# Block 1 after its attention: down weights staged earlier, first shared inputs split earlier, weight conversions set between the shared items

## What is computed

```python
xn = _layernorm(x)
s = _L1_attn_ref(xn, ...)     # 16 heads, causal softmax with ALiBi, out @ w_proj + b_proj
g = _silu(_L1_ffn_ref(xn, ...))
x = x + s * g

# _L1_ffn_ref: E = 16 experts of inner width 176, top 2 of a sigmoid router,
# and one shared expert of inner width 352 that every token passes
y0 = _mlp(xf, sw1, sw2, sw3)                  # (silu(x @ w1.T) * (x @ w3.T)) @ w2.T
for e1, e2, e3, we in experts: y = y + _mlp(xf, e1, e2, e3) * we[:, None]
```

## Time and profile before

| stretch of the span (us) | what runs | PE busy | ACT busy | DVE busy | mean granted clock |
|---|---|---|---|---|---|
| 0 to 337.0 | block 0 | 298.7 | 137.9 | 181.2 | 1.00 to 120 us, 0.95 behind |
| 337.0 to 568.9 | projections and attention of block 1 | 188.9 | 98.0 | 136.0 | 0.92 |
| 568.9 to 601.1 | tail of the last sequence, shared expert on chunk 0 | 18.2 | 12.4 | 11.0 | 0.79 |
| 601.1 to 668.0 | routed experts, first part | 66.0 | 51.6 | 44.4 | 0.97 |
| 668.0 to 745.5 | last experts, shared expert on chunks 1 to 3, combination, store | 43.9 | 31.1 | 47.8 | 0.81 |

### The profile page before, as it was taken

One profiled execution on the slowest core, in us unless ns is written; L12 is line 12 of the kernel. 1 busy time (PEld: TensorE's weight loads), 2 busy tenths in 40 slices (PEclk: granted clock), 3 DMA queues, 4 the chain that ended last, 5 costly groups with the idle time before them and its releaser, 6 DMA issues.

```text
span 745.5 us, 12625 instructions
## 1 busy us (share of the span) xinstructions
PE 615.7 (83%) x4090; PEld 481.1 (65%) x4090; DVE 420.4 (56%) x1000; ACT 331.1 (44%) x715; POOL 158.8 (21%) x164
## 2 busy tenths in 40 slices
PE   3989982999999989895728999998887589999750
PEld 2868872999988878783414666666665267776430
DVE  6166663455545374558686546555441356665468
ACT  2223321566554344433412544543444458886331
POOL 0136660000005434006002122222000100001652
PEclk9999997899999999997858999999999799999885
DMA  9904434334315111009296757658300425552324
GB/s 326 295 35 141 152 125 168 99 115 119 117 65 182 50 51 49 9 1 187 85 139 140 157 134 163 133 118 147 47 2 1 121 85 157 164 157 84 95 87 138
DMA packets 85179, 86.50 MB, mean 116 GB/s; under 512 B 19435, under 2 KB 76654, under 8 KB 84846
## 3 DMA queue, kind: packets, MB, share of 16 engines
q1 hardware_dynamic: 78462, 68.79, 35.8%
q0 software_dynamic: 6144, 16.79, 7.6%
q10 hardware_dynamic: 512, 0.13, 0.1%
HBM read 51.20 MB, written 34.21 MB: 115 GB/s over the span
## 4 chain that ended last, share of the span: by engine, by line
PE 39%; DVE 10%; ACT 5%; issue 3%; DMA 2%; POOL 0%; ACTq 0%; SPq 0%; DVEq 0%
PE bank L793 5%; PE bank L856 4%; PE bank L880 3%; PE bank L948 3%; PE bank L1015 3%; PE bank L1033 3%; PE bank L992 2%; PE bank L642 2%; PE bank L844 2%; PE bank L811 2%; PE bank L1017 2%; PE bank L994 2%; PE bank L867 1%; PE bank L972 1%; DVE mneg L1853 1%
## 5 line engine op out<-in xcount | busy, mean ns | idle before, releaser
L575 POOL DMA_INDIRECT slots<-xn,slot_of x64 | 66.4, 1037 | 183.5 <-DMA slots<-xn,slot_of 110.4
L1853 DVE TENSOR_REDUCE mneg<-bank 128x2 f32<-128x512 f32 (+1 forms) x96 | 62.5, 685 | 41.7 <-PE bank L994 41.2
L1690 DVE TENSOR_TENSOR xgl<-bank,xgh 128x256 f16<-128x256 f32 (+1 forms) x86 | 36.5, 424 | 51.2 <-ACT xgh L1276 51.2
L588 POOL DMA_INDIRECT rets<-results,slot_of x32 | 33.5, 1048 | 147.3 <-DMA results<-ys 105.9
L1664 DVE TENSOR_TENSOR hf<-bank,sg 128x512 f32<-128x512 f32 x36 | 24.6, 690 | 65.5 <-PE bank L793 60.4
L588 POOL DMA_INDIRECT gu<-results,slot_of x32 | 31.3, 978 | 121.2 <-DMA results<-ys 104.6
L844 PE MATMUL bank<-cf,xn 128*128 128x128 f32 x172 | 35.9, 292 | 14.6 <-DMA xn<-slots 12.4
L992 PE MATMUL bank<-KS,QS 99*128 99x256 bf16 (+1 forms) x256 | 37.2, 254 | 12.8 <-DVE mneg L1853 7.5
L1251 ACT ACTIVATE sg<-bank 128x512 f32<-128x512 f32 x36 | 21.2, 599 | 57.1 <-PE bank L793 57.0
L1697 DVE TENSOR_TENSOR hs<-bank,gs 128x176 f32<-128x176 f32 x86 | 29.3, 341 | 28.8 <-ACT gs L1282 24.5
L1385 ACT ACTIVATE exps_first_keys<-bank 128x512 f32<-128x512 f32 x64 | 34.7, 597 | 21.8 <-PE bank L1017 21.8
(11 more groups left out here) (234 smaller groups left out, 1637.1 us busy)
## 6 DMA issues: line engine op xcount, KB each, us to landing
xn<-slots SPq DMA_DIRECT2D x86, 128.0 KB, 2.2
results<-ys SPq DMA_DIRECT2D x86, 128.0 KB, 1.7
projection_parts<-parts SPq DMA_DIRECT2D x16, 384.0 KB, 3.2
QS<-projection_parts SPq DMA_DIRECT2D x48, 128.0 KB, 4.4
KS<-projection_parts SPq DMA_DIRECT2D x48, 128.0 KB, 6.5
slots<-zrow SPq DMA_DIRECT2D x1, 6016.0 KB, 23.8
x<-in_x SPq DMA_DIRECT2D x8, 512.0 KB, 5.9
x<-in_w SPq DMA_DIRECT2D x4, 704.0 KB, 8.1
```

The lines of the kernel that those rows point to most:

```text
L575: pool.indirect_dma_start(out=slots_dram, out_offset=bass.IndirectOffsetOnAxis(ap=at, axis=0), in_=xn[:, t, :], in_offset=None).then_inc(s ...
L588: pool.indirect_dma_start(out=rets[L][:, t % RETS, r, :], out_offset=None, in_=results_dram[L], in_offset=bass.IndirectOffsetOnAxis(ap=at, ...
L1690: dve.tensor_tensor(xgl[L][:, j % 2, :], PS[j % 2][:, 0:D], high[:, j % 2, :], ALU.subtract)\
L1853: dve.tensor_reduce(mneg[:, qt, h0:h0 + heads], PS[6 + p % 2][:].rearrange("p (n k) -> p n k", n=heads), AX.X, ALU.max, negate=True).then_ ...
```

## The change

Four things are moved, and nothing is computed otherwise.

- `dn_stage` gets four buffers and a place in SBUF where `QS`/`KS` of slot 2 lay (last used by sequence 5). SP issues all four pairs as soon as the transposed scores of sequences 0 to 5 are formed. The experts' first rows, which stand behind them in SP's queue, move along.
- `high_x(1, 0)` and `low_x(1, 0)` stand inside round 7 of the attention on ACT and DVE, and `shared_gates(1, 0)` stands on PE behind round 7 and ahead of the tail of the last sequence.
- POOL clears `dn1` after the last weighted values instead of after the last projection.
- The conversions stand between the shared items: on each engine its two L1454-like ones (128 partitions) behind item 0, its two L1455-like ones (48 partitions) behind item 1, and the split of chunk 1 (`high_x(1, 1)`, `low_x(1, 1)`) behind item 2.

```diff
-            sp.wait_ge(s_ps[1], after(NSEQ))
+            sp.wait_ge(st_ps, after(12 * (NSEQ - 2)))
             for n in range(4):
-                if n >= 2:
-                    sp.wait_ge(dn_act if n % 2 == 0 else dn_dve, n // 2)
                 e = slice(4 * n, 4 * n + 4)
-                sp.dma_start(dn_stage[:, n % 2, :, 0:D], w1_rows[0:P, e, 2 * KT * P:WCOLS]).then_inc(s_stage[n % 2], 16)
...
+                sp.dma_start(dn_stage[:, n, :, 0:D], w1_rows[0:P, e, 2 * KT * P:WCOLS]).then_inc(s_stage[n], 16)
...
             scatter(1, 1)
+            pool.wait_ge(pv_ps, after(4 * NSEQ))
+            pool.memset(dn1.bitcast(F32)[:, :, 1, :], 0.0).then_inc(dn_zero, 1)
             pool.wait_ge(s_ps[1], after(NSEQ))
             pool.memset(hs1[:, :, INNER:D], 0.0).then_inc(pads_set, 1)
-            pool.memset(dn1.bitcast(F32)[:, :, 1, :], 0.0).then_inc(dn_zero, 1)
...
             for u in range(-1, NSEQ):
                 attention(u)
+            pe.wait_ge(s_sw, 16)
+            shared_gates(1, 0)
             pe.wait_ge(s_sb[1], after(NSEQ - 1))
             heads_transposes(NSEQ - 1, 0)
...
-            shared(1, (0,), nothing)
+            shared(1, (0,), nothing, begun=True)
...
                     exp_scores(u, 3)
+                if not ahead:
+                    high_x(1, 0)
...
             outputs_copy(NSEQ - 1)
-            act.wait_ge(s_ps[1], after(NSEQ))
-            high_x(1, 0)
-            high_x(1, 1)
-            act.wait_ge(dn_zero, 1)
-            for n in (0, 2):
-                act.wait_ge(s_stage[n % 2], 32 * (n // 2 + 1))
...
+            def down_weights(k):
+
+                if k < 2:
+                    for n in (0, 2):
+                        act.wait_ge(s_stage[n], 32)
+                        if k == 0:
+                            act.activation(dn1[:, 4 * n:4 * n + 4, 0, :], dn_stage[:, n, :, 0:D], ACT.Copy)
+                        else:
+                            act.wait_ge(dn_zero, 1)
+                            act.activation(dn1[0:INNER - P, 4 * n:4 * n + 4, 1, :],
+                                           dn_stage[0:INNER - P, n, :, D:2 * D], ACT.Copy).then_inc(dn_act, 1)
+                else:
+                    high_x(1, 1)
+
+            shared(1, (0,), down_weights)
+            act.wait_ge(scattered[1], 16 * 2 * NTOK)
             experts(1, nothing)
...
                     result(1, u - 1, TAIL_BANK, r1[:])
+                if not ahead:
+                    low_x(1, 0)
```

More of the change, by code:

```diff
@@ L269, in two_block_kernel @@
         inner, tb = scope(block1)
-        dn_stage = tb("dn_stage", [P, 2, 4, 2 * D], BF16)
         dn1 = tb("dn1", [P, E1, 2, D], F32R)
@@ L273, in two_block_kernel @@
         xl16 = tb("xl16", [P, 2, KT, CH], F16)
+        dn_stage = tb("dn_stage", [P, 4, 4, 2 * D], BF16)
         sg1 = tb("sg1", [P, 2, CH], F32)
@@ L352, in two_block_kernel @@
         s_gu, s_sw = sem("gate_up_landed_1"), sem("shared_landed_1")
-        s_stage = [sem(f"down_stage_landed_{n}") for n in range(2)]
+        s_stage = ring("down_stage_landed", 4)
         dn_zero, dn_act, dn_dve, sd_set = sem("down_zeroed"), sem("down_act"), sem("down_dve"), sem("shared_down_set")
@@ L535, in _ @@
             w1_rows = w1_in.rearrange("n p c -> (n p) c")[0:ROWS[1], :].rearrange("(e i) c -> i e c", i=INNER)
-            sp.wait_ge(s_ps[1], after(NSEQ))
+            sp.wait_ge(st_ps, after(12 * (NSEQ - 2)))
             for n in range(4):
-                if n >= 2:
-                    sp.wait_ge(dn_act if n % 2 == 0 else dn_dve, n // 2)
                 e = slice(4 * n, 4 * n + 4)
-                sp.dma_start(dn_stage[:, n % 2, :, 0:D], w1_rows[0:P, e, 2 * KT * P:WCOLS]).then_inc(s_stage[n % 2], 16)
-                sp.dma_start(dn_stage[0:INNER - P, n % 2, :, D:2 * D], w1_rows[P:INNER, e, 2 * KT * P:WCOLS])\
-                  .then_inc(s_stage[n % 2], 16)
+                sp.dma_start(dn_stage[:, n, :, 0:D], w1_rows[0:P, e, 2 * KT * P:WCOLS]).then_inc(s_stage[n], 16)
+                sp.dma_start(dn_stage[0:INNER - P, n, :, D:2 * D], w1_rows[P:INNER, e, 2 * KT * P:WCOLS])\
+                  .then_inc(s_stage[n], 16)
             expert_rows(1)
@@ L820, in shared_down_low, with shared @@
                 mm.then_inc(s_down, 1)
-            def shared(L, chunks, between):
+            def shared(L, chunks, between, begun=False):
                 items = [SHARED[L] * c + n for c in chunks for n in range(SHARED[L])]
-                shared_gates(L, items[0])
+                if not begun:
+                    shared_gates(L, items[0])
                 waiting = None
@@ L1141, in _ @@
             pe.wait_ge(s_sb[1], after(NSEQ))
-            pe.wait_ge(s_sw, 16)
             pe.wait_ge(sd_set, 1)
@@ L1447, in _ @@
             outputs_copy(NSEQ - 1)
-            act.wait_ge(s_ps[1], after(NSEQ))
-            high_x(1, 0)
-            high_x(1, 1)
-            act.wait_ge(dn_zero, 1)
-            for n in (0, 2):
-                act.wait_ge(s_stage[n % 2], 32 * (n // 2 + 1))
-                act.activation(dn1[:, 4 * n:4 * n + 4, 0, :], dn_stage[:, n % 2, :, 0:D], ACT.Copy)
-                act.activation(dn1[0:INNER - P, 4 * n:4 * n + 4, 1, :], dn_stage[0:INNER - P, n % 2, :, D:2 * D],
-                               ACT.Copy).then_inc(dn_act, 1)
-            act.wait_ge(scattered[1], 16 * 2 * NTOK)
             def nothing(k):
                 pass
-            shared(1, (0,), nothing)
+            def down_weights(k):
[12 more added lines that the diff above has]
+            act.wait_ge(scattered[1], 16 * 2 * NTOK)
             experts(1, nothing)
@@ L1915, in _, with down_weights @@
             result(1, NSEQ - 1, TAIL_BANK, r1[:])
-            dve.wait_ge(s_ps[1], after(NSEQ))
-            low_x(1, 0)
-            low_x(1, 1)
-            dve.wait_ge(dn_zero, 1)
-            for n in (1, 3):
-                dve.wait_ge(s_stage[n % 2], 32 * (n // 2 + 1))
-                dve.tensor_copy(dn1[:, 4 * n:4 * n + 4, 0, :], dn_stage[:, n % 2, :, 0:D])
-                dve.tensor_copy(dn1[0:INNER - P, 4 * n:4 * n + 4, 1, :], dn_stage[0:INNER - P, n % 2, :, D:2 * D])\
-                   .then_inc(dn_dve, 1)
             def nothing(k):
                 pass
+            def down_weights(k):
+                if k < 2:
+                    for n in (1, 3):
+                        dve.wait_ge(s_stage[n], 32)
+                        if k == 0:
+                            dve.tensor_copy(dn1[:, 4 * n:4 * n + 4, 0, :], dn_stage[:, n, :, 0:D])
+                        else:
+                            dve.wait_ge(dn_zero, 1)
+                            dve.tensor_copy(dn1[0:INNER - P, 4 * n:4 * n + 4, 1, :],
+                                            dn_stage[0:INNER - P, n, :, D:2 * D]).then_inc(dn_dve, 1)
+                else:
+                    low_x(1, 1)
             def combine_chunk(c):
```

## The result

The changed kernel takes 738.07 us (median of 4 runs, 735.37 to 738.69), the kernel before 745.77 us on the same chip (4 runs, 742.55 to 747.39). The ratio is 0.9887, with an interval of 0.986 to 0.9913: 7.7 us less. The forecast was 736.4 us, in a range from 732.8 to 742.0. The profiled execution took 738.69 us; before it was 747.37, so 8.7 us less there. By its interval the gain is clear of no change, and it stays under 2%.

The account below looks back on a forecast made before the run. Bound: a stage with no engine near full, its chain waiting on clearing, conversions, a late transfer and a table load. Experts 10.9 us earlier, less 0.5, 0.4 and 0.5, gives 9.5: from 745.89 to 736.4 us, range 732.8 to 742.0.

Parts of the forecast that it names:

- The gates of item 0 and their price: PE ahead of the tail: gates start about 569.35, take 1.74 us, and the tail starts 2.15 us later.
- The tail: Last sequence's tail through the projection: 7.1 us instead of 7.8, half the clock's 1.45 us regained; bounds 7.8 and 6.35.
- Items 0 and 1: Shared expert after the tail: item 1's gate half done about 580.0, table load off the chain; experts eventually start at 590.2.
- rival 1: PE runs the shared expert's stage at 1.2 GHz: 4.2 us lost, gain 5.3, 740.6 us; chance 0.20.
- the prediction's own signs of being wrong: Maxima wait over 3 us, gates of item 1 in 3.4 us, or the experts' stage itself longer than before.
- the prediction's signs: Expected signs included experts 10 to 11 us earlier relative to the last exponentials, and gates of item 0 near 569.4.
- What is given back ahead of the experts: Split of chunk 1 ahead of the first expert tile costs about 0.5 us; PE starting experts less busy costs 0.4.
- The transfers and the maxima: Early transfers from SP meet the maxima of sequence 6, which PE waits for: 0.5 us lost, bounds 0 and 3.7.
- rival 2: Maxima of sequence 6 wait behind the staged transfers: 3.7 us instead of 0.5, gain 6.3, 739.6 us; chance 0.12.
- The table load: ACT's load before the first silu: 1.28 us leaves the chain; a further drain of about 1.38 us left out.
- Rival 3: Slower than before: transfers flow at only 129 GB/s, maxima served last, 10.4 us lost against 10.0 gained, 746.3; chance 0.03.
- Rival 4: More clock: projection wholly at 2.4 GHz, experts' start as before, no maxima wait, ACT overlaps; gain 12.5, 733.4; chance 0.05.

Follow-up runs that it names:

- The edit that takes the price away: Changed kernel with the gate products of item 0 in two halves between the transposes of the last sequence's tail; 743.07 us, ratio 0.9826, stage 19.32.
- the second execution: The changed kernel again, unaltered, on a second chip; 746.13 us, ratio 0.9891, stage 21.38.
- the third: The changed kernel once more, unaltered, beside the last group of runs; 734.69 us, ratio 0.9873, stage 23.01.
- both edits of the transfers' issue: Changed kernel with SP's transfers issued to meet the maxima of sequence 6 (751.13 us), or held until those maxima landed (735.11 us).
- all three: Changed kernel with item 0's gates and the conversions in the tail's waits, and transfers behind the maxima of sequence 6; 728.04 us, ratio 0.9761.

## Why the prediction was right, point by point

**The gates of item 0 and their price.** Forecast: start 569.35, tail 2.15 us later. Measured, with the 0.28 us of the start added: 569.31, and the tail at 571.04 instead of 568.95, 2.09 later. The edit that takes the price away gains 2.06 us. That this is a real loss was right, and its size to the tenth.

**The tail.** Forecast 7.1 us, as the gates ahead would make PE busier. Measured 579.35 - 570.76 = 8.6 us, beyond my upper bound of 7.8, since the last transposes (1.11 us against 0.66) were slow too. In the second execution it took 587.60 - 581.24 = 6.4, my lower bound. No execution of the changed kernel showed the 7.1 (the third took 8.0); the middle is a mean over two levels of the clock. The reason that I gave for it, gates ahead of the tail, is neither refuted nor shown. The last projection took 3.4 to 3.6 us in all four traces without gates ahead of the tail or in its waits (both of the kernel before, the transfers alone, the gates behind). With the gates ahead it took 3.3 to 3.8 us in three traces (the changed kernel's first and third, the conversions ahead) and 1.99 in three (its second, both edits of the transfers' issue). With products in the tail's waits it took 1.98 or 1.99 in all four. That speaks for work in the waits as what keeps the clock, and for gates ahead as half a help, but so few traces don't settle it. Why one tail falls and its twin, with the same program on PE, doesn't, stays open.

**Items 0 and 1.** Forecast: gate half of item 1 at 580.0. Measured 582.0 (582.3 with the 0.28), behind the tail's 1.4 us and gates at 1.2 GHz. This is the gate half of rival 1, 0.9 us; its other prices, item 0's gates, item 2's gates and the down products, didn't occur. Gates of item 1 in 3.4 us were among the prediction's own signs of being wrong, and in this execution they took 3.59; in the second and third they ran at 2.4 GHz. From here on all ran as worked out: silu 2 forecast 3.2 us behind silu 1, measured 3.3; the high part of item 2 was held up by ACT's conversions as forecast; down products, 1.09 and the start to the experts alike. In place of 590.2 the experts started at 592.24 + 0.28 = 592.5: 2.3 us late, all of it the clock's. So the stage became 8.6 us shorter here, not the 10 to 11 of the prediction's signs. By the other executions it is 21.38, 23.01 and, in the two kernels that differ only in when SP issues, 21.37 and 21.36; with 24.83 the mean of the five is 22.4, where the forecast was 590.2 - 567.69 = 22.5. That agreement is of a mean between two levels of the clock; no trace showed 22.5.

**What is given back ahead of the experts.** Forecast 0.5 and 0.4. The first gate product of the experts in the kernel before, and in the changed one:

```profile
602.70 0.47 PE L856 MATMUL bank<-gu,xgh 128*128 x2 [0.47 <-ACT xgh L1276]
```

```profile
594.34 0.77 PE L856 MATMUL bank<-gu,xgh 128*128 x2 [0.99 <-DVE xgl L1698]
```

The first stands 1.56 us behind the experts' start, the second 2.10, behind DVE's `xgl`, which had `low_x(1, 1)` ahead of it: 0.54 us, as forecast. Of the whole rest the first pair of traces shows only 0.2 us lost. Over all of them it is 143.4 and 144.4 before, 144.6, 145.4 and 144.6 in the changed kernel: 1.0 us between the means, against a forecast of 0.9. But the two traces of the kernel before differ by 1.0 themselves, so the clock's part of 0.4 is neither shown nor refuted.

**The transfers and the maxima.** Forecast 0.5, bounds 0 to 3.7. Lost in round 6: 0 in the first execution, 2.8 and 0.5 in the next. The value was a fair middle, but one step behind it failed: I let the row tiles be issued with the pairs at 526. They wait for the scatters, the last of which was issued at 535.55, not at 522.31 as in the earlier trace rows. By then the pairs had all but landed (241 GB/s between 532 and 534, 23 between 534 and 536), and the maxima, issued at 533.45, met only their end. That the first execution lost nothing was thus luck of POOL's timing, not foreseen. In the second, PE's wait of 3.02 us is over the 3 us that the prediction had named as a sign of rival 2.

It needn't be the row tiles. In the kernel with gates and conversions in the tail's waits the row tiles left only when PE was already at work, and PE still waited 2.65 us, 1.0 too much. What was in flight were pairs, issued until 540.88, and a scatter:

```profile
542.65 1.15 ACTq L1414 DMA_DIRECT2D QS<-mT  x2
546.10 0.39 PE L1016 MATMUL bank<-QS,KS 101*128 101x256 bf16 x2 [2.65 <-DMA QS<-mT]
548.10 2.73 SPq L451 DMA_DIRECT2D xn<-slots  x6
```

All traces side by side, sorted by what the queues moved from 0.5 to 2 us behind the issue of the maxima (11 GB/s is a stretch with nothing beside them):

| trace | GB/s | issue to PE's start (us) | round 6 (us) | row tiles issued, against the maxima |
|---|---|---|---|---|
| kernel before (two), transfers behind the maxima, all three | 11 | 2.45 to 2.46 | 20.59 | none, or behind PE's start |
| conversions ahead | 18 | 2.46 | 20.59 | 5.6 us behind |
| products that compute nothing | 19 | 2.45 | 20.58 | 1.4 behind |
| gates in the tail's waits | 22 | 2.45 | 20.59 | 6.9 behind |
| changed kernel, first | 31 | 2.48 | 20.61 | 4.5 behind |
| changed kernel, third | 86 | 2.96 | 21.08 | 2.3 behind |
| gates behind the tail | 161 | 2.98 | 22.57 | 0.2 ahead |
| gates and conversions in the waits | 177 | 3.45 | 21.58 | 5.5 behind |
| transfers at the maxima | 228 | 5.04 | 25.21 | 2.0 behind |
| changed kernel, second | 282 | 3.81 | 23.41 | 1.6 ahead |
| transfers and clearing alone | 326 | 3.93 | 23.52 | 2.9 ahead |

The delay follows the bytes in flight, with one trace out of line, the one in which the transfers went on longest. In four traces (5.04, 3.93, 3.81 and 2.98 us) TensorE's clock fell to 0.50 in the wait or behind it, and round 6 lost 1.4 to 2.0 us on top of the wait; with 3.45 and 2.96 it stayed at 1.00, and nothing was added. So the mechanism of rival 2 is real, with 0.5 to 2.6 us of added wait, below the prediction's upper bound of 3.7.

From what the Trainium skill says in "DMA: Bandwidth & Descriptors", section on queues, rings and completion order, that a DMA engine takes turns between the queues that have work, a packet at a time, the prediction had concluded that the maxima would pay next to nothing. The runs don't bear that conclusion out: 8 KB paid up to 2.6 us.

**The table load.** 1.28 us, and the silu 0.01 us behind it (576.81). The drain of about 1.38 us that the Trainium skill adds in "ScalarE: Activation LUTs", section on what a table load costs, shows in none of the 13 traces in which the silu could follow at once, so leaving it out of the sum was right.

**The sum.** Forecast 9.5 us. Measured in the profiled execution: stage 8.6 (10.9 forecast, 2.3 lost to the clock), maxima 0 (0.5), given back 0.2 (0.9), and 0.3 ahead of it all: 8.7. Errors of 2.3 one way and 1.5 the other nearly cancel, and that is luck. By medians it is 7.7, 8.3 and 11.4 us on the three occasions; by the ratios (0.9887, 0.9891, 0.9873) it is 8.4, 8.2 and 9.5, the last with an interval from 6.7 to 12.3. The edit with the transfers alone splits the stage: 5.4 us are the wait, 2.2 the clock behind it. Against its 25.87 the rest of the change (split, table load, conversions between, less the price of the gates) brought 1.0 to 4.5 us, as the tail's clock was low or full. Rival 3 did not occur. Rival 4's 12.5 us lies just beyond the third occasion's interval, and no trace has all of its parts.

## What to carry to other kernels

Work that is moved ahead of a chain of small steps delays the whole chain by its length; the same work placed in the waits between those steps cost nothing here, and this alone turned 21.4 us into 19.3, with the conversions alike 18.3. A load that is issued early must be checked for what its issue really waits for. A small transfer that an engine waits for should find no large one still in flight; by the table it is the bytes moving beside it that count, not which was issued first. Where one execution shows products at half speed, look at a second of the same kernel before a gain or a loss is put down to an edit.

## What the runs showed that I had not expected

The clock fell in the kernel before at the same places in both traces, the second of them behind waits of PE of 6.92 and 6.84 us, but in the changed kernel's tail in two executions of three, with the same instructions and the same waits of 0.69 to 0.88 us: 3.78, 1.99 and 3.60 us for one projection.

Two transfers of 8 KB that were 1.3 us in flight behind their issue took 3.9 us among transfers of 96 KB and more.

Clearing on POOL beside a split on DVE cost nothing: `low_x` took 1.21 us with the memset alongside (567.67, POOL's clearing from 567.96) and 1.23 us at 592.53 with POOL idle. The 1.22 of the earlier trace rows is no figure without it: there too the clearing ran alongside (splits from 577.90 to 580.26, clearing from 577.00 to 580.46).
